# Attention with two-part float32r scores on array halves, and ten shared-expert batches between its steps

## The chip, the core and the metric

One NeuronCore of a Trainium2 runs the whole program. Its engines are TensorE (PE in the profile, its weight loads PEld), VectorE (DVE), ScalarE (ACT), GpSimd (POOL) and SyncE (SP, which only issues transfers). Each works through its own instructions in order and waits on semaphores. The metric is the device time of one execution in microseconds; lower is better.

## The reference

A gated cross attention and then a gated mixture of experts, on 32 batches of 128 rows by 512 columns (8 heads, 8 routed experts of which each token takes 2, and one shared expert), all in float32:

```python
q, k, v = proj(layernorm(x)), proj(ctx), proj(ctx)        # per batch, head size 16, sequence 512
attn = softmax(q @ k.T / 4)                               # 8 heads, 512 x 512
x = x + tanh(g_xattn) * (attn @ v)
h = rmsnorm(layernorm(x)) * rms_weight                    # 4096 tokens of 512
probs = softmax(h @ router_w); topv, topi = top_k(probs, 2); topv /= sum(topv)
moe = sum over the two experts e of topv[e] * (silu(h @ w_gate[e]) * (h @ w_up[e])) @ w_down[e]
sh = (silu(h @ sw_gate) * (h @ sw_up)) @ sw_down
out = x + tanh(g_ffn) * (moe + sh)
```

## The kernel before, in words

**Attention.** The main loop runs over turns i = -3 .. 31 and in each over 32 steps s (8 heads x 4 key tiles). In turn i, TensorE issues at step s one score matmul for the exponentials of batch i (`exp_scores`, L1033: keys on partitions, out to a bank of a ring of three, read by ScalarE in `exponential`, L892) and one for the row maxima of batch i+1 (`max_scores`, L1011: queries on partitions, out to another ring of three, read by VectorE in `maximum`, L696). float32 accuracy comes from splitting q and k into three bf16 parts stacked over the rows of the array: six products of 16 rows, 96 rows, and two more rows that subtract the maximum (98). At each step with s % 4 == 2 come four matmuls of probabilities with values (`values`, L1062, float32, each on 32 array columns). A float32 matmul stands in the trace as two instructions.

Other pieces stand at fixed steps and share one bank, `misc_ps`: projections of k and q of batch i+3 at steps 22 and 26 and of v of batch i+2 at step 7 (`project`, L996, L1000); transposes of the maxima at steps 18 and 2 (`turn_maxima`, L1020); the transpose of the tokens of batch i-3 and its router product at steps 10 and 14 (L1038, L1049).

**The parts.** ScalarE evacuates a projection and casts the high part, GpSimd subtracts for the middle and the low one (`split`, L523 to L526), SyncE writes the parts to DRAM and reads them back stacked.

**The denominators.** After the last value group of a batch, at step 2 of the next turn, ScalarE copies the sums (`take_values`, L899), SyncE stores them (`store_values`, L376), loads the denominators back spread over the partitions (L382), VectorE inverts them at step 13 (`invert`, L690), SyncE stores these (L386) and loads them with the sums for GpSimd (L392, L393), which adds the attention to x (`add_attention`, L533 to L535). GpSimd also refines inverse square roots by Newton steps (L503 to L505), normalises x (L514) and makes the tokens (`tokens`, L555, L556); SyncE stores these and their transposes to DRAM.

**The stage behind.** Jobs j = 0 .. 102: 32 shared-expert jobs, one a batch (16 gate and up matmuls, L1135, and the down product, L1160), then 71 routed jobs of 128 gathered tokens (L1140, L1148, L1160). During the shared jobs VectorE computes the routing in pieces, one a job; GpSimd scatters 64 columns of token numbers into a map in DRAM (L590), SyncE reads it back at job 28 (L483), TensorE transposes it at job 29 (L1100), and with these numbers GpSimd gathers tokens (L596). SyncE loads the routed experts' weights one at every second job from 5 on (L443).

The order is written out by hand: the constants at the top of the file give the steps and jobs.

## Time and profile before

| | us |
|---|---|
| median of 3 runs (lowest, highest) | 1590.97 (1590.81, 1591.98) |
| span of the profiled execution, first to last instruction | 1525.5 |
| TensorE busy in it | 1475.7 |
| GpSimd, VectorE, ScalarE busy | 814.5, 887.8, 782.5 |

The profile is of one execution. Busy time of an engine is the union of its instructions; where they overlap in its pipeline, starts are closer together than the length of one. "Idle before, releaser" is the time in which an engine waited ahead of a group, and whose end let it go. The chain of waits is followed back from the last instruction.

### The profile page before, as it was taken

To read this page: it belongs to the slowest core of one execution; us is meant where nothing else is said; L and a number is where in the kernel's file an instruction comes from. 1 tells how busy PE (TensorE), PEld (TensorE's weight loads), DVE (VectorE), ACT (ScalarE), POOL (GpSimd) and SP (SyncE) were. 2 spreads that over 40 slices of the span, in tenths; PEclk is the share of its full clock that TensorE was granted. 3 is DMA by queue.
4 is the path that set the end of the run, shared out by engine and by line. 5 is a ranking of instruction groups with operands and counts; after the bars stand their busy time and mean duration, and the time that the engine had idled before them with its cause. 6 is when DMAs were issued, how large, how long until landed. Compare 5 with 4: busy or idle time off the path is not lost.

```text
span 1525.5 us, 23419 instructions
## 1 busy us (share of the span) xinstructions
PE 1475.7 (97%) x7362; PEld 669.8 (44%) x7362; DVE 887.8 (58%) x1802; ACT 782.5 (51%) x1531; POOL 814.5 (53%) x1241
## 2 busy tenths in 40 slices
PE   5999999999999999999999999989999999999997
PEld 1233333333333333333333328767755454545443
DVE  5888888888888888888888842512221121211111
ACT  2577777777777777777777771100022222222221
POOL 6346675766757667576674443375134444444442
PEclk9999999999999999999999999999999999999999
DMA  6566667766676666765666424785345455554554
GB/s 153 128 160 168 175 167 183 180 161 162 162 177 163 168 163 162 178 170 152 165 154 167 117 92 162 248 213 121 113 76 97 85 96 88 93 91 88 92 90 61
DMA packets 159304, 215.10 MB, mean 141 GB/s; under 512 B 28162, under 2 KB 102416, under 8 KB 158160
## 3 DMA queue, kind: packets, MB, share of 16 engines
q1 hardware_dynamic: 137136, 175.78, 44.9%
q0 software_dynamic: 17952, 37.30, 14.0%
q8 instruction: 62, 1.02, 0.3%
q10 hardware_dynamic: 4096, 0.53, 0.2%
q14 instruction: 58, 0.48, 0.1%
HBM read 126.12 MB, written 86.91 MB: 140 GB/s over the span
## 4 chain that ended last, share of the span: by engine, by line
PE 87%; DMA 6%; DVE 2%; issue 1%; POOL 1%; ACT 1%; SPq 1%; ACTq 0%; POOLq 0%; DVEq 0%
PE bank L1140 16%; PE bank L1062 16%; PE bank L1033 14%; PE bank L1011 14%; PE bank L1160 10%; PE bank L1135 5%; PE bank L996 4%; PE bank L1038 3%; DMA arena<-ht_d 2%; PE bank L1049 2%; PE bank L1000 2%; DMA pv_d<-arena 1%; PE bank L1148 1%; DVE row_max L696 1%; PE bank L1020 1%
## 5 line engine op out<-in xcount | busy, mean ns | idle before, releaser
L696 DVE TENSOR_REDUCE row_max<-bank 128x1 f32<-128x512 f32 x1024 | 664.9, 682 | 111.6 <-PE bank L1011 102.5
L892 ACT ACTIVATE arena<-bank 128x512 f32<-128x512 f32 x1024 | 564.5, 612 | 205.5 <-PE bank L1033 194.0
L1011 PE MATMUL bank<-arena 96*128 96x512 bf16 x1024 | 392.2, 384 | 7.8 <-DVE row_max L696 5.5
L1033 PE MATMUL bank<-arena 98*128 98x512 bf16 x1024 | 387.2, 380 | 2.9 <-ACT arena L892 1.8
L1062 PE MATMUL bank<-arena 128*32 128x512 f32 x2048 | 272.7, 605 | 1.0 <-ACT arena L892 0.7
L1140 PE MATMUL bank<-arena 128*128 x568 | 255.5, 592 | 0.0
L834 DVE TENSOR_TENSOR arena<-arena,bank 128x256 f32<-128x256 f32 x103 | 43.4, 421 | 331.7 <-ACT arena L943 327.9
L943 ACT ACTIVATE arena<-bank 128x256 f32<-128x256 f32 x103 | 39.6, 384 | 378.2 <-PE bank L1140 224.9
L604 POOL DMA_INDIRECT out<-xs,ids x71 | 112.3, 1581 | 226.3 <-ACT xs L954 184.0
L1160 PE MATMUL bank<-arena 128*128 (+1 forms) x412 | 193.8, 593 | 0.9 <-ACT arena L959 0.9
L523 POOL TENSOR_TENSOR arena<-arena 128x512 bf16<-128x512 f32 x62 | 71.6, 1155 | 226.7 <-ACT arena L884 224.0
L1033 PEld LDWEIGHTS bank<-arena 98*128 98x128 bf16 x1024 | 102.2, 100 | 184.4 <-ACT arena L892 90.5
L1011 PEld LDWEIGHTS bank<-arena 96*128 96x128 bf16 x1024 | 100.2, 98 | 142.4 <-DVE row_max L696 80.7
L1140 PEld LDWEIGHTS bank<-arena 128*128 128x128 f32 x568 | 102.4, 190 | 101.9 <-issue 101.9
L1135 PE MATMUL bank<-arena 128*128 128x128 f32 x1024 | 121.9, 278 | 8.4 <-DMA arena<-ht_d 8.4
L1135 PEld LDWEIGHTS bank<-arena 128*128 128x128 f32 x1024 | 119.9, 194 | 21.2 <-DMA arena<-ht_d 13.0
L1160 PEld LDWEIGHTS bank<-arena 128*128 128x128 f32 x412 | 75.8, 190 | 84.4 <-issue 84.4
L822 DVE COPY arena<-bank 128x512 f32<-128x512 f32 x71 | 49.1, 691 | 104.3 <-PE bank L1038 104.3
L596 POOL DMA_INDIRECT xs<-h_d,ids x71 | 69.6, 980 | 56.1 <-DVE wts L862 34.8
L954 ACT ACTIVATE xs<-bank,wts 128x512 f32<-128x512 f32 x71 | 48.8, 687 | 95.5 <-PE bank L1160 56.8
L996 PE MATMUL bank<-arena 128*128 128x512 f32 x128 | 76.6, 682 | 15.8 <-POOL arena L514 9.7
L590 POOL DMA_INDIRECT map_d<-meta,slots x64 | 61.6, 962 | 50.1 <-DVE slots L805 30.9
(122 smaller groups left out, 1252.4 us busy)
## 6 DMA issues: line engine op xcount, KB each, us to landing
arena<-parts_q SPq DMA_DIRECT2D x64, 256.0 KB, 4.8
pv_d<-arena SPq DMA_DIRECT2D x32, 512.0 KB, 6.3
parts_k<-arena SPq DMA_DIRECT2D x96, 128.0 KB
arena<-parts_k SPq DMA_DIRECT2D x32, 384.0 KB, 4.9
parts_q<-arena SPq DMA_DIRECT2D x96, 128.0 KB
arena<-in_w SPq DMA_DIRECT2D x8, 1536.0 KB, 8.9
h_d<-arena SPq DMA_DIRECT2D x33, 256.0 KB, 6.7
out<-xs SPq DMA_DIRECT2D x33, 256.0 KB, 2.5
```

The costliest lines, as they stand in the source:

```text
L523: nc.gpsimd.tensor_tensor(mid, proj[n], hi, ALU.subtract).then_inc(s_part, 1)
L596: nc.gpsimd.indirect_dma_start(gathered[i % IN_RING], None, h_d, bass.IndirectOffsetOnAxis(ap=ids[:, i:i + 1], axis=0)).then_inc(s_got[i % ...
L604: nc.gpsimd.indirect_dma_start(out_d, bass.IndirectOffsetOnAxis(ap=ids[:, i:i + 1], axis=0), y_sb[i % OUT_RING], None, compute_op=ALU.add) ...
L696: nc.vector.reduce_max(row_max[b % 2][:, u:u + 1], m_ps[(STEPS * b + u) % M_BANKS][:], AX_X).then_inc(s_mx, 1)
L892: nc.scalar.activation(probs[group % 3][:, j, :], e_ps[n % E_BANKS][:], ACT.Exp, scale=float(DH) ** -0.5).then_inc(s_exp, 1)
L996: nc.tensor.matmul(misc_ps[:], (wk, wq)[n][:], ctx_in[b % 2] if n == 0 else xn[b % 2], start=True, stop=True).then_inc(s_proj, 1)
L1011: nc.tensor.matmul(m_ps[n % M_BANKS][:], q_stack[b % 3][0:STACK, h, qt * P:(qt + 1) * P], k_stack[b % 3][0:STACK, h, :], start=True, stop= ...
L1033: nc.tensor.matmul(e_ps[n % E_BANKS][:], k_stack[b % 3][0:SHIFTED, h, kt * P:(kt + 1) * P], q_stack[b % 3][0:SHIFTED, h, :], start=True, s ...
L1062: last = nc.tensor.matmul(pv_ps[2 * DH * j:2 * DH * (j + 1), :], v_ones[b % 3][:, kt, GROUP * g + j, :], probs[pair % 3][:, j, :], start=( ...
L1135: last = nc.tensor.matmul(G_PS[j % 2][:, f * P:(f + 1) * P], w_shared[:, c, f * P:(f + 1) * P], h_t[j % 3][:, c, :], start=(c == 0), stop= ...
L1140: last = nc.tensor.matmul(G_PS[j % 2][:], h_t[j % 3][:, c, :], routed_weights(j, c), start=(c == 0), stop=(c == CHUNKS - 1))
L1160: last = nc.tensor.matmul(Y_PS[j % 2][:], act_t[j % 2][:, f, :], w, start=(f == 0), stop=(f == FF // P - 1))
```

## The change

- Scores: q and k are split into two float32r parts (high and low). Three products of 16 rows are 48 rows (50 with the rows of the maximum), which fit in half of the array. Of a pair of heads one lies on partitions 0 to 63, the other on 64 to 127. At each step the exponentials' matmul takes one half and the maxima's the other.
- Bank rings per reader: `misc_ps` no longer serves the attention's pieces. Projections and token transposes take banks of the exponentials' ring (read by ScalarE), transposed maxima and router products banks of the maxima's ring (read by VectorE). Dictionaries `e_at` and `m_at` number their uses.
- Shared expert of batches 0 to 9 (`FUSED = 10`): in turns 3 to 12, the 16 gate and up matmuls stand in eight pieces of two at steps 7 to 17 and the down product in four at steps 24 to 29, in `misc_ps`. ScalarE takes a tanh and two copies, GpSimd four operations (silu is computed from tanh), SyncE stores the result. The stage behind has 22 shared jobs (`NS`), the map is read at job 19 and transposed at job 20, weights are loaded one a job. x is held for 22 batches.
- The maxima's rows go from VectorE (one negation) over GpSimd (two small operations) and SyncE's queue, before from VectorE (two) and ScalarE's queue. GpSimd makes the high part too, in place of ScalarE.
- SyncE's order in a turn is new, and the steps of the pieces are.

```diff
-K_PARTS = (HI, MID, LO, HI, MID, HI)
-Q_PARTS = (HI, HI, HI, MID, MID, LO)
+K_PARTS = (HI, LO, HI)
+Q_PARTS = (HI, HI, LO)
...
+PAIR = 2
+READS = PAIR * (len(runs(K_PARTS)) + len(runs(Q_PARTS)))
 STACK = len(K_PARTS) * DH
+SIDE = P // PAIR
...
+PROJECT_AT = {20: (3, 0), 28: (3, 1), 3: (2, 2)}
+MAX_AT = (19, 4)
 VALUES_LATE = 2
+TURN_TOKENS_AT = 1
+LOGITS_AT = 5
+GATE_UP_AT = {7: 2, 9: 2, 11: 2, 12: 2, 13: 2, 15: 2, 16: 2, 17: 2}
+DOWN_AT = (24, 25, 27, 29)
+HIDDEN_AT = 18
+SHARED_AT = 30
+MOMENTS2_AT = 3
 MOMENTS_AT = 23
 RECIP_AT = 13
+FUSED = 10
...
+        JOBS = NS + NT
+
+        EXPERT_JOBS = range(5, 5 + EXPERTS - 1)
...
+        LATE_AT = EXPERT_JOBS.stop + 2
+        MAP_AT = NS - 3
+        TURN_AT = NS - 2
...
             def split(b, n):
+                pool.wait_ge(s_er, e_at["project", b, n] + 1)
+                pool.wait_ge(s_wr[n], 2 * DMA * b)
+                hi, lo = parts[n]
+                nc.gpsimd.tensor_scalar(hi[:], proj[n], 1.0, 0.0, ALU.mult, ALU.add).then_inc(s_hi, 1)
                 pool.wait_ge(s_hi, 2 * b + n + 1)
...
+                nc.gpsimd.tensor_tensor(lo[:], proj[n], hi[:].bitcast(F32), ALU.subtract).then_inc(s_lo, 1)
...
+            def maxima_rows(b, half):
+                pool.wait_ge(s_mr, m_at["turn", b, half] + 1)
...
+                link(nc.gpsimd.tensor_scalar(rows[:, 0, :], m_neg[half][:], 1.0, 0.0, ALU.mult, ALU.add))
+                nc.gpsimd.tensor_tensor(rows[:, 1, :], m_neg[half][:], rows[:, 0, :].bitcast(F32), ALU.subtract
+                                        ).then_inc(s_mm, 1)
+
+            def activate_shared(b):
+                pool.wait_ge(s_ft, b + 1)
+                pool.wait_ge(s_fc, b + 1)
+                link(nc.gpsimd.tensor_scalar(half_tanh[:], half_tanh[:], 1.0, 0.5, ALU.add, ALU.mult))
+                link(nc.gpsimd.tensor_tensor(half_tanh[:], half_tanh[:], gate_and_up[:, 0:FF], ALU.mult))
...
             for i in TURNS:
                 if is_b(i + 2) and i + 2 > 0:
+                    split(i + 2, 0)
                     split(i + 2, 1)
+                if is_b(i):
+                    maxima_rows(i, 1)
+                if fused(i - 4):
+                    add_shared(i - 4)
                 if is_b(i + 4):
                     normalise(i + 4)
                 if is_b(i - 2):
                     tokens(i - 2)
-                if is_b(i + 3) and i + 3 > 0:
-                    split(i + 3, 0)
+                if is_b(i + 1):
+                    maxima_rows(i + 1, 0)
+                if fused(i - 3):
+                    activate_shared(i - 3)
                 if is_b(i - 1):
                     add_attention(i - 1)
...
+            def take_hidden(b):
+                act_e.wait_ge(s_fg, b + 1)
...
+                nc.scalar.activation(half_tanh[:], misc_ps[:, 0:FF], ACT.Tanh, scale=0.5).then_inc(s_ft, 1)
+                nc.scalar.copy(gate_and_up[:], misc_ps[:]).then_inc(s_fc, 1)
+
+            def take_shared(b):
+                act_e.wait_ge(s_fd, b + 1)
...
+                nc.scalar.activation(y_shared[:], misc_ps[:], ACT.Copy, scale=tgates[:, 1:2]).then_inc(s_fo, 1)
...
+            def next_e(at):
+                if at >= E_BANKS:
+                    pe.wait_ge(s_er, at - E_BANKS + 1)
+                return e_ps[at % E_BANKS]
+
+            def next_m(at):
+                if at >= M_BANKS:
+                    pe.wait_ge(s_mr, at - M_BANKS + 1)
+                return m_ps[at % M_BANKS]
...
             def max_scores(b, u):
...
+                p, qt, e = u // (PAIR * KT), u // PAIR % KT, 1 - u % PAIR
+                rows = slice(e * SIDE, e * SIDE + STACK)
...
+                ps = next_m(m_at["max", b, u])
+                nc.tensor.matmul(ps[:], q_stack[b % 3][rows, p, qt * P:(qt + 1) * P],
+                                 k_stack[b % 3][rows, p, :], start=True, stop=True).then_inc(s_mf, 1)
...
             def exp_scores(b, s):
                 g, kt, j = s // (GROUP * KT), s // GROUP % KT, s % GROUP
...
+                p, e = GROUP // PAIR * g + j // PAIR, j % PAIR
+                rows = slice(e * SIDE, e * SIDE + SHIFTED)
...
+                ps = next_e(e_at["exp", b, s])
+                nc.tensor.matmul(ps[:], k_stack[b % 3][rows, p, kt * P:(kt + 1) * P],
+                                 q_stack[b % 3][rows, p, :], start=True, stop=True).then_inc(s_ef, 1)
...
+            def shared_hidden(b, units):
...
+                for unit in units:
+                    f, c = divmod(unit, CHUNKS)
+                    last = nc.tensor.matmul(misc_ps[:, f * P:(f + 1) * P], w_shared[:, c, f * P:(f + 1) * P],
+                                            tok_t[:, c, :], start=(c == 0), stop=(c == CHUNKS - 1))
```

How the orders move, at three places. The first is TensorE at steps 7 to 10 of a turn in which a shared batch is worked in. Before (L1033 exponentials, L1011 maxima, L1000 projection of v, L1062 values, L1038 tokens):

```order
L1033 MATMUL bank1<-arena 128x512
L1011 MATMUL bank3<-arena 128x512
L1000 MATMUL bank7<-arena 128x128 x4
L1033 MATMUL bank2<-arena 128x512
L1011 MATMUL bank4<-arena 128x512
L1033 MATMUL bank0<-arena 128x512
L1011 MATMUL bank5<-arena 128x512
L1033 MATMUL bank1<-arena 128x512
L1011 MATMUL bank3<-arena 128x512
L1062 MATMUL bank6<-arena 32x512 x4
L1038 MATMUL bank7<-ident,arena 128x128 x4
```

After (L1141 exponentials, L1120 maxima, L1184 gate and up, L1209 values):

```order
L1141 MATMUL bank2<-q_stack0,k_stack0 128x512
L1120 MATMUL bank3<-k_stack1,q_stack1 128x512
L1184 MATMUL bank7<-arena 128x128 x2
L1141 MATMUL bank0<-q_stack0,k_stack0 128x512
L1120 MATMUL bank4<-k_stack1,q_stack1 128x512
L1141 MATMUL bank1<-q_stack0,k_stack0 128x512
L1120 MATMUL bank5<-k_stack1,q_stack1 128x512
L1184 MATMUL bank7<-arena 128x128 x2
L1141 MATMUL bank2<-q_stack0,k_stack0 128x512
L1120 MATMUL bank3<-k_stack1,q_stack1 128x512
L1209 MATMUL bank6<-arena 32x512 x4
```

The projection and the tokens have gone to steps 3 and 1, and two pieces of the shared expert, on all 128 rows, stand between scores that now take 64 rows each.

The second is SyncE from the store of the sums to the load of the denominators. Before (L367 reads of k, L376 store of the sums, L357 writes of q's parts, L382 load of the denominators, L386 store of their inverses):

```order
L367 DMA arena<-parts_k1 16x8x512
L376 DMA pv_d<-arena 128x2x512
L357 DMA parts_q1<-arena 8x16x512
L382 DMA arena<-pv_d 128x1x32
L357 DMA parts_q1<-arena 8x16x512
L386 DMA rden_d<-arena 128x32
```

After (L396 write of a part, L418 store of the sums, L374 and L369 loads of the next inputs, L453 rows of the maxima, L409 reads of k, L424 load of the denominators):

```order
L396 DMA parts_q1<-q_lo 8x16x512
L418 DMA pv_d<-arena 128x2x512
L374 DMA arena<-in_ctx 128x512
L369 DMA xs<-in_x 128x512
L453 DMA q_stack0<-m_rows1 2x8x128 x2
L409 DMA k_stack2<-parts_k1 32x4x512 x2
L409 DMA k_stack2<-parts_k1 16x4x512 x2
L424 DMA arena<-pv_d 128x1x32
```

The store has gone behind all writes of parts, and between it and the load stand two inputs, the rows of the second half's maxima and four reads of k.

The third is the end of SyncE's turn. Before (L386 store of inverses, L332 input, L403 transposed tokens, L367 reads of q, L392 and L393 loads for the attention sum, L397 store of tokens):

```order
L386 DMA rden_d<-arena 128x32
L357 DMA parts_q1<-arena 8x16x512
L332 DMA arena<-in_ctx 128x512
L403 DMA ht_d<-arena 128x512
L367 DMA arena<-parts_q1 16x8x512 x2
L367 DMA arena<-parts_q1 32x8x512 x2
L392 DMA arena<-rden_d 128x1x512
L393 DMA arena<-pv_d 128x1x512
L397 DMA h_d<-arena 128x512
```

After (L458 store of a finished shared batch, L428 store of inverses, L439 store of tokens, L434 and L435 loads for the attention sum, L453 rows of the first half's maxima):

```order
L458 DMA out<-xs 128x512
L428 DMA rden_d<-arena 128x32
L439 DMA h_d<-arena 128x512
L434 DMA arena<-rden_d 128x1x512
L435 DMA arena<-pv_d 128x1x512
L453 DMA q_stack1<-m_rows0 2x8x128 x2
```

The store of the tokens now stands ahead of the loads for the attention sum, and the rows of the maxima have come onto this queue.

## Rows read from the trace of the kernel before

**Rows 1.** the page: span, busy us (share) by engine, one group (busy us, mean ns)

```profile
span 1525.5 us, 23419 instructions
...
PE 1475.7 (97%) x7362; PEld 669.8 (44%) x7362; DVE 887.8 (58%) x1802; ACT 782.5 (51%) x1531; POOL 814.5 (53%) x1241
...
L696 DVE TENSOR_REDUCE row_max<-bank 128x1 f32<-128x512 f32 x1024 | 664.9, 682 | 111.6 <-PE bank L1011 102.5
```

**Rows 2.** table by stretch: us; PE, PEld, DVE, ACT, POOL busy; clock; DMA

```profile
500.00:600.00 100.00, 99.95 (x559) 36.46 (x559) 85.98 (x177) 76.96 (x148) 64.50 (x111) 1.00 0.67 169
```

**Rows 3.** timeline of TensorE in one turn: start us, length us, what, how many

```profile
501.71 0.38 PE L1011 MATMUL bank<-arena 96*128 96x512 bf16 x1
502.02 1.07 PE L1062 MATMUL bank<-arena 128*32 128x512 f32 x8
503.02 0.28 PE L1020 MATMUL bank<-ident,row_max 128*16 128x128 f32 x1
...
530.16 0.28 PE L1020 MATMUL bank<-ident,row_max 128*16 128x128 f32 x1
```

**Rows 4.** the chain of waits in the same turn: start us, us, what

```profile
504.60 0.22 PE bank L1033
...
505.04 1.00 PE bank L1062 x8
506.04 1.06 PE bank L996 x2
...
513.63 0.32 PE bank L1033
```

**Rows 5.** the chain of waits behind the turns, shared jobs to first routed

```profile
914.94 3.59 PE bank L1135 x32
...
927.57 5.51 DMA arena<-pv_d
...
1041.71 3.57 PE bank L1135 x32
1045.28 1.72 PE bank L1160 x4
...
1084.03 0.18 PE bank L1100 x2
...
1101.01 3.44 PE bank L1140 x8
```

**Rows 6.** timeline of ScalarE in the turn: five exponentials back to back

```profile
513.67 2.58 ACT L892 ACTIVATE arena<-bank 128x512 f32<-128x512 f32 x5
```

**Rows 7.** timeline of VectorE in the turn: reciprocals and maxima

```profile
499.71 0.35 DVE L690 RECIPROCAL arena<-arena 128x32 f32<-128x32 f32 x1 [0.62 <-DMA arena<-pv_d]
...
514.21 2.48 DVE L696 TENSOR_REDUCE row_max<-bank 128x1 f32<-128x512 f32 x4 [0.23 <-PE bank L1011]
...
526.15 0.34 DVE L690 RECIPROCAL arena<-arena 128x32 f32<-128x32 f32 x1
```

**Rows 8.** timeline of SyncE in the turn: store of values, load of denominators

```profile
518.03 0.38 SPq L376 DMA_DIRECT2D pv_d<-arena  x1
...
524.03 0.61 SPq L382 DMA_DIRECT2D arena<-pv_d  x1
```

**Rows 9.** timeline of GpSimd in the turn: idle, big operations, start of normalising

```profile
510.24 1.15 POOL L523 TENSOR_TENSOR arena<-arena 128x512 bf16<-128x512 f32 x1 [6.14 <-ACT arena L884]
...
515.20 0.77 POOL L534 TENSOR_SCALAR arena<-arena,tgates,tg_bv 128x512 f32<-128x512 f32 x1
516.04 1.27 POOL L535 TENSOR_TENSOR xs<-xs,arena 128x512 f32<-128x512 f32 x1
...
521.00 0.34 POOL L503 TENSOR_SCALAR newton<-rstd,arg 128x1 f32<-128x1 f32 x1
...
524.35 0.77 POOL L514 TENSOR_SCALAR arena<-xs,rstd,nmr 128x512 f32<-128x512 f32 x1
```

**Rows 10.** the scatters into the map: ns min/median/max, first and last start us

```profile
L590 POOL DMA_INDIRECT map_d<-meta,slots x64: 954/958/1236, 975.5 to 1055.3; - x64
```

## What the change does to the time: the prediction

> **What bounds the kernel now.** Read the page first [rows 1]: TensorE is busy 97% of a 1525.5 us span. Busy matmuls prove little, so next comes one table by stretches [rows 2]: from 500 to 600 us TensorE is busy all the time at the full granted clock, VectorE 86%, ScalarE 77%, GpSimd 65%. Then one period of the attention loop (a turn): the transpose of the first half of the next batch's maxima starts at 503.02, that of the next turn at 530.16 [rows 3], so a turn takes 27.14 us, and 31 of the 32 take that (the last has no next batch to take maxima for). The chain of waits says of what [rows 4]: a score matmul costs 0.22 us, a group of eight value instructions 1.00. 64 score matmuls at 0.218 make 14.0 us; the other 13.2 are eight value groups, three projections, the transposes of maxima and tokens, and the router. Nothing waits in between. Behind the turns come 32 shared jobs at 3.57 + 1.72 = 5.29 us [rows 5] and then 71 routed jobs, which the change leaves alone.
>
> The median is 1590.97 us, the profiled span 1525.5; the 65.5 us between lie outside the span and are taken as unchanged, so every difference below is added to 1590.97.
>
> **The scores.** The count stays at 64 a turn and the columns at 512. What changes is the type (bf16 to float32r) and the rows: 48 or 50, at partition 0 or 64, and each exponential's matmul stands beside a maximum's on the other half. No row shows a float32r matmul. Nearest from below is the bf16 one, 0.22 us; from above the float32 projection of 512 columns, 1.06 us with its switch, in two instructions [rows 4]. Nor does a row show two array halves at work together, but the values show the like for columns: eight instructions of 512 columns on four 32-column strips take 1.00 us, where two such instructions alone take 1.06, so strips do overlap. I take the near end, 0.22 us a matmul and two at once: 32 x 0.22 = 7.0 us a turn in place of 14.0. Ends for the range: 14.0 (halves one after the other, or half rate), and 64 x 1.06 / 2 = 34.
>
> The Trainium skill, Perfetto Trace Analysis, Engine Utilization, halves the array's rate only for FP32_LOW_HIGH among four-byte types; that is for the near end, and no row here shows it.
>
> **Switches.** Into a value group the step is 0.31 us instead of 0.22 (501.71 to 502.02) [rows 3], and the matmul behind one costs 0.32 [rows 4]: 0.19 a round trip. Score matmuls now use half the rows, so every full-array piece between them makes such a trip too: 7 a turn (three projections, two maxima, tokens, router): 1.3 us. TensorE then needs 7.0 + 13.2 + 1.3 = **21.5 us** in a plain turn.
>
> The rule that speaks against the change is in TensorEngine Tiling (Array Packing), Tiling Modes, of the Trainium skill: changing the mode, not just the tile, drains the array. The 0.09 and 0.10 above agree in kind. If a drain instead exposed all of a matmul's 0.38 us beyond its 0.22 [rows 3], a trip would cost 0.32, a turn with shared pieces 19 x 0.13 = 2.5 us more, and the sum would end 25 us later.
>
> **The shared expert moved in.** Ten of 31 turns take in one shared batch: 5.3 us of matmuls, in 8 + 4 pieces, so 12 more trips (2.3). TensorE: 21.5 + 5.3 + 2.3 = **29.1 us**. ScalarE gets three activations more there and loses two casts in every turn; it is busy 0.77 x 27.14 = 21 us of a turn now, and back to back five exponentials take 2.58 us [rows 6], so that it stays below 29.
>
> **What is late next: VectorE.** One maximum lasts 0.68 us [rows 1], but four back to back end after 2.48, so a next one comes every (2.48 - 0.68) / 3 = 0.60 us [rows 7]. 32 of them 19.2, two statistics over as many columns 1.3, a reciprocal 0.35, and the negations and small ones about 1.6 (an estimate, at most what is left of the 86% of 27.14 us after 32 x 0.60): **22.4 us**. So in a plain turn TensorE (21.5) hands the bound to VectorE.
>
> **The denominators.** Then a path shows that 27.14 us hides. It starts with the last value group of the batch before (step 2), runs through ScalarE's copy, SyncE's store of the values, its load of the denominators, and ends in VectorE's reciprocal, which stands at step 13 ahead of all later maxima. Times [rows 4, 7, 8]: values 1.0, copy 0.6 (as an exponential), store 6.0 (518.03 to 524.03), load 2.1 (524.03 to 526.15), reciprocal 0.35: 10.1 us. The reciprocal at 499.71 already waited 0.62 us for it. From step 13 to the next step 2 VectorE has 21 maxima (12.6), a negation and a set of moments (1.4): 14.0. Together 24.1 us, above VectorE's 22.4. The store now also stands behind the four writes of parts, and the load behind the maxima's rows and four reads of k, all on SyncE.
>
> **GpSimd's loop.** Its order closes a second loop, since SyncE stores the tokens ahead of the loads for the attention sum. From [rows 9]: two splits, each a scalar operation and a subtraction with the gaps between, 2 x (0.8 + 1.4) = 4.4; rows of maxima about 0.8 (an estimate, two operations at 0.34 for a tiny one); normalising 3.35 + 0.8 = 4.1; tokens 3.35 + 0.8 + 1.3 = 5.4; then three issues and a landing (0.4 + 0.6 + 5.5 [rows 5]) 6.5, beside which lie the next rows and the activation; adding attention 2 x 1.27 + 0.77 and gaps, 3.6. Sum 24.8 us. Before, this loop was not closed: GpSimd sat idle 6.14 us ahead of 510.24. The two loops meet at the store (it waits for the second split), which I put at half a microsecond. Plain turn: **25.3 us**. Fused turn: the pieces lengthen steps 2 to 13 by about 3 us, so both paths hide under TensorE: 29.1 + 0.2 = **29.3**.
>
> 31 turns before: 31 x 27.14 = 841. After: 21 x 25.3 + 10 x 29.3 = 531 + 293 = 824. **17 us gained.** Filling the pipeline (memsets of 2048 columns that lie under the first loads, one part less to split) and the last turn: 0, bounds -5 and +5.
>
> **The stage behind.** Ten jobs less are 53 us of matmuls, but a path of other work ends last there. GpSimd issues 64 scatters from 975.5 to 1055.3, 1.27 us each [rows 10]; the last ends 141 us after the first shared matmul at 914.94; its landing and the map's load take 5 more. From the map's transposes to the first routed matmul there are two jobs, a gather and so on: 1084.03 to 1101.01, 17 us [rows 5]. 146 + 17 = 163 us against 186 before. SyncE's load of the map stands ahead of the tokens of jobs 20 and 21, so TensorE stands idle there, about 20 us. The weight loads come every job instead of every second: +2. So **21 us gained**, not 53.
>
> Sum: 17 + 21 = 38, and 1590.97 - 38 = **1553 us**.
>
> **Rivals.**
> - Quick: the paths through SyncE and GpSimd don't bind, and switches are cheap. Plain 23.0, fused 28.0: 841 - 763 = 78, + 21: 1492 us. For: landing times of 2.1 us in the loads; against: the wait of 0.62 us that is there already.
> - Slower, the halves take turns (or four-byte rows go in at half rate): the scores stay at 14.0 us. Plain 14.0 + 13.2 + 1.3 = 28.5, fused 36.1: 841 to 959, + 118 - 21: 1688 us; with free switches (27.14 and 32.4) 1623. Middle 1660. It decides from 0.34 us a pair on: there plain turns take 14.5 + 32 x 0.34 = 25.4 and fused 33.0, and 10 x 5.9 - 21 x 1.7 = 23 eats the gain behind the turns. For: the values overlap in columns, never in rows, and no row has a four-byte operand at one pass. Against: nothing else in the trace.
> - SyncE late: landings grow as more bytes fall into a shorter turn, plain 27: 841 - 860, 21 gained behind: 1589 us.
> - float32r priced as float32: 34 + 14.5 a turn, over 2200 us.
>
> **How the numbers follow.** Forecast 0.50 (1515 to 1585), quick 0.15, turns taken 0.25, SyncE late 0.06, float32 price 0.04. The range 1470 to 1665 leaves out a twentieth below and some 0.13 above. Within 0.2% (3 us, what a measurement can tell): 0.03, from where the forecast and the late SyncE reach the old time. Slower 0.30, faster 0.67.
>
> **What would show it.** Pairs of score matmuls with starts close together and a new pair each 0.22 us (right) or single ones 0.22 apart (the slower rival). Plain turns near 25 with VectorE waiting for a DMA at its reciprocal; fused ones near 29 with TensorE full. Behind the turns one long idle stretch of TensorE until the map lands, and 163 us from the first shared to the first routed matmul. Plain turns at 23 would refute both loops; fused turns over 31 the price of a switch.

## The result, and the profile after

The changed kernel takes 1765.47 us (median of four runs), the kernel before 1590.89 on the same chips: 1.107 times as long, 95% interval 1.101 to 1.113. The ratio leaves out the slowest of the four executions (1782.72 us), which lies over 1.5% above the fastest. **Slower by 11%**, where 1553 us were forecast and 1665 was the upper end.

The page of the kernel after, against [rows 1]; its first lines, then TensorE's busy tenths and its granted clock in 40 slices of 44 us:

```profile
span 1750.0 us, 23258 instructions
PE 1576.1 (90%) x7402; PEld 739.2 (42%) x7402; DVE 877.2 (50%) x1716; ACT 780.6 (45%) x1487; POOL 795.4 (45%) x1347
PE   3999999999999998998899899994198999999997
PEclk7688997999998787798888999996599999999999
```

TensorE is busy 100 us longer than before, although it now does 32 pairs a turn in place of 64 single score matmuls. And its clock, full in [rows 2], is now below nine tenths in 14 of the first 26 slices.

Matmuls of a fused turn at full clock (start, length, engine, line; L1141 makes the exponentials' scores, L1120 the maxima's, L1184 is a gate and up piece, L1209 a value group):

```profile
430.92 0.50 PE L1141 MATMUL bank<-q_stack,k_stack 50*128 50x512 f32 x1
430.92 0.50 PE L1120 MATMUL bank<-k_stack,q_stack 48*128 48x512 f32 x1
431.35 0.71 PE L1184 MATMUL bank<-arena 128*128 128x128 f32 x4
432.00 0.50 PE L1141 MATMUL bank<-q_stack,k_stack 50*128 50x512 f32 x1
...
436.61 0.49 PE L1141 MATMUL bank<-q_stack,k_stack 50*128 50x512 f32 x1
436.62 0.73 PE L1120 MATMUL bank<-k_stack,q_stack 48*128 48x512 f32 x2
436.95 0.40 PE L1141 MATMUL bank<-q_stack,k_stack 50*128 50x512 f32 x1
437.28 1.06 PE L1209 MATMUL bank<-arena 128*32 128x512 f32 x8
438.27 0.49 PE L1141 MATMUL bank<-q_stack,k_stack 50*128 50x512 f32 x1
```

The two matmuls of a pair start together, so the halves do overlap. But the next pair starts 0.34 us later (436.61 to 436.95), not 0.22, and a pair alone between two pieces on the full array takes 0.43 (430.92 to 431.35). The piece then takes 0.65 for four matmuls of 128 columns.

The 0.34 is the price of the first pair behind a piece only. Where three pairs stand in a row (L1146 transposes tokens), the first takes 0.33 us (515.81 to 516.14) and the second 0.24 (to 516.38):

```profile
514.81 1.06 PE L1209 MATMUL bank<-arena 128*32 128x512 f32 x8
515.81 0.49 PE L1141 MATMUL bank<-q_stack,k_stack 50*128 50x512 f32 x1
515.81 0.73 PE L1120 MATMUL bank<-k_stack,q_stack 48*128 48x512 f32 x2
516.14 0.64 PE L1141 MATMUL bank<-q_stack,k_stack 50*128 50x512 f32 x2
516.38 0.40 PE L1120 MATMUL bank<-k_stack,q_stack 48*128 48x512 f32 x1
517.08 0.63 PE L1146 MATMUL bank<-ident,arena 128*128 128x128 f32 x4 [0.30 <-ACT arena L981]
```

Over all pairs at full clock from 150 to 1000 us the medians are 0.234 us for a further pair ahead of a pair, 0.338 for the first one behind a piece, 0.330 for a further one ahead of a piece and 0.431 for one alone between two pieces. So a pair costs 0.234, and a piece adds 0.10 to the pair behind it and 0.10 to the pair ahead of it.

A plain turn:

```profile
662.01 0.79 PE L1141 MATMUL bank<-q_stack,k_stack 50*128 50x512 f32 x1
662.01 1.22 PE L1120 MATMUL bank<-k_stack,q_stack 48*128 48x512 f32 x2
662.60 1.05 PE L1141 MATMUL bank<-q_stack,k_stack 50*128 50x512 f32 x2
665.27 1.38 PE L1120 MATMUL bank<-k_stack,q_stack 48*128 48x512 f32 x2 [1.62 <-DVE row_max L789]
665.87 0.62 PE L1141 MATMUL bank<-q_stack,k_stack 50*128 50x512 f32 x1
666.59 1.93 PE L1209 MATMUL bank<-arena 128*32 128x512 f32 x8
```

Here the value group takes 1.86 us (to 668.45), against 1.00 at full clock, and TensorE waits for a bank that VectorE has not read. VectorE's rows tell why (waits over eleven turns, 565.3 to 932.9: total, times, longest):

```profile
DVE row_max L789 <- PE bank L1120: 84.2, 109, 2.0
DVE arena L782 <- DMA arena<-pv_d: 25.4, 9, 7.6
```

L782 is the reciprocal: it waited 0.62 us before [rows 7], now up to 7.6. The same eleven turns by stretches (us, busy and count of TensorE, its weight loads, VectorE, ScalarE, GpSimd, then clock, DMA share, GB/s):

```profile
565.30:932.90 367.60, 336.69 (x1691) 130.49 (x1693) 254.39 (x506) 221.53 (x415) 177.99 (x374) 0.83 0.55 143
```

A plain turn is 33.4 us, where it was 27.1.

**Where the 160 us lie.** A second profile of the kernel before (e0 below) has a span of 1589.6 us, in which the first shared matmul stands at 916.9 and the first routed one at 1165.2. After: 1117.6 and 1326.2. So attention is 200.6 us longer, the shared jobs 39.6 shorter (208.7 for 248.3), the routed part the same (423.8 for 424.4): 160.4, the difference of the spans.

Within attention, from reciprocal to reciprocal: the first comes 13.6 us later (clock at half from 19 to 77). Eleven periods up to 497.2 take 389.7 us where 11 x 27.1 = 298 stood; the next sixteen, to 1025.5, take 528.3 against 434. The last four are 3 us longer.

### The profile page after: what moved, and what is told of

Its sections match the earlier page's. It is cut to its first block and busy times, and to the rows that moved or that the text cites. A ratio compares the mean times of both kernels' runs of the same rounds, so it can differ in the third digit from the quotient of the medians.

```text
span 1750.0 us, 23258 instructions
## 1 busy us (share of the span) xinstructions
PE 1576.1 (90%) x7402; PEld 739.2 (42%) x7402; DVE 877.2 (50%) x1716; ACT 780.6 (45%) x1487; POOL 795.4 (45%) x1347
## 5 line engine op out<-in xcount | busy, mean ns | idle before, releaser
L1120 PE MATMUL bank<-k_stack,q_stack 48*128 48x512 f32 x1024 | 476.1, 522 | 44.7 <-DVE row_max L789 33.4
L1141 PE MATMUL bank<-q_stack,k_stack 50*128 50x512 f32 x1024 | 454.3, 504 | 12.3 <-ACT arena L981 11.4
L1141 PEld LDWEIGHTS bank<-q_stack,k_stack 50*128 50x128 f32 x1024 | 190.9, 205 | 400.4 <-ACT arena L981 276.5
L1209 PE MATMUL bank<-arena 128*32 128x512 f32 x2048 | 312.0, 685 | 0.8 <-ACT arena L981 0.7
L1120 PEld LDWEIGHTS bank<-k_stack,q_stack 48*128 48x128 f32 x1024 | 194.4, 207 | 77.8 <-DVE row_max L789 61.4
L1052 ACT ACTIVATE arena<-bank 128x256 f32<-128x256 f32 x93 | 35.6, 383 | 403.3 <-PE bank L1293 225.0
L1313 PE MATMUL bank<-arena 128*128 (+1 forms) x372 | 178.7, 602 | 8.0 <-issue 7.1
L599 POOL TENSOR_SCALAR m_rows<-m_neg 16x128 fp32r<-16x128 f32 x64 | 18.4, 288 | 359.7 <-issue 181.2
L1288 PE MATMUL bank<-arena 128*128 128x128 f32 x704 | 96.3, 291 | 54.7 <-issue 53.4
L1293 PEld LDWEIGHTS bank<-arena 128*128 128x128 f32 x568 | 102.4, 190 | 101.9 <-issue 101.9
L1288 PEld LDWEIGHTS bank<-arena 128*128 128x128 f32 x704 | 91.4, 206 | 66.0 <-issue 62.5
L1313 PEld LDWEIGHTS bank<-arena 128*128 128x128 f32 x372 | 70.0, 193 | 89.0 <-issue 89.0
L1106 PE MATMUL bank<-arena 128*128 128x512 f32 x128 | 86.1, 760 | 17.1 <-POOL arena L574 12.1
```

The costliest lines, as they stand in the source:

```text
L1106: nc.tensor.matmul(ps[:], (wk, wq)[n][:], ctx_in[b % 2] if n == 0 else xn[b % 2], start=True, stop=True).then_inc(s_ef, 1)
L1120: nc.tensor.matmul(ps[:], q_stack[b % 3][rows, p, qt * P:(qt + 1) * P], k_stack[b % 3][rows, p, :], start=True, stop=True).then_inc(s_mf, 1)
L1141: nc.tensor.matmul(ps[:], k_stack[b % 3][rows, p, kt * P:(kt + 1) * P], q_stack[b % 3][rows, p, :], start=True, stop=True).then_inc(s_ef, 1)
L1209: last = nc.tensor.matmul(pv_ps[2 * DH * j:2 * DH * (j + 1), :], v_ones[b % 3][:, kt, GROUP * g + j, :], probs[pair % 3][:, j, :], start=( ...
L1288: last = nc.tensor.matmul(G_PS[j % 2][:, f * P:(f + 1) * P], w_shared[:, c, f * P:(f + 1) * P], h_t[j % 3][:, c, :], start=(c == 0), stop= ...
L1293: last = nc.tensor.matmul(G_PS[j % 2][:], h_t[j % 3][:, c, :], routed_weights(j, c), start=(c == 0), stop=(c == CHUNKS - 1))
```

## The experiments

All fifteen in one table. "Attention" is the start of the first shared matmul, "fused" and "plain" are mean periods of the reciprocal over six turns with and eleven turns without shared pieces, and the clock is the mean over these eleven (1.00 is 2.4 GHz, 0.50 is 1.2 GHz). The last column is the kernel before on the same chip.

| kernel | us | attention | fused | plain | clock | before |
|---|---|---|---|---|---|---|
| after | 1751.8 | 1117.6 | 36.0 | 33.4 | 0.83 | |
| e0 before again | 1591.4 | 916.9 | | 27.1 | 1.00 | 1584.3 |
| e1 reciprocal late | 1799.5 | 1167.1 | 35.6 | 33.7 | 0.87 | 1584.3 |
| e2 one half only | 2627.9 | | 73.5 | 56.1 | 0.50 | 1584.3 |
| e3 full rows | 1726.4 | 1093.3 | 34.3 | 32.5 | 0.97 | 1584.3 |
| e4 bfloat16 halves | 1706.8 | 1072.6 | 32.6 | 32.7 | 0.89 | 1585.8 |
| e5 load first | 1782.8 | 1151.2 | 35.2 | 33.9 | 0.85 | 1585.8 |
| e6 full rows, load first | 1745.6 | 1112.5 | 34.4 | 33.9 | 0.96 | 1585.8 |
| e7 sixteen fused | 1750.5 | 1148.9 | 36.2 | (33.9, mixed) | 0.92 | 1585.8 |
| e8 no trip | 1659.4 | 1058.9 | 35.5 | 28.5 | 0.98 | 1533.9 |
| e9 full rows, no trip | 1635.7 | 1037.0 | 34.4 | 29.2 | 1.00 | 1533.9 |
| e10 rows first | 1715.1 | 1117.4 | 35.6 | 32.2 | 0.88 | 1533.9 |
| e11 bfloat16, rows first | 1676.5 | 1077.2 | 33.3 | 32.5 | 0.87 | 1533.9 |
| e12 before, half the scatters | 1551.2 | 916.4 | | 27.2 | 1.00 | 1588.5 |
| e13 bfloat16, no trip | 1630.1 | 998.7 | 32.6 | 29.1 | 0.93 | 1588.5 |
| e14 after again | 1761.1 | 1129.9 | 36.2 | 33.6 | 0.84 | 1588.5 |

Each row is one execution; the two profiles of the changed kernel (after, e14) lie 12 us apart in attention. Whole times compare only on one chip: that of e8 to e11 runs the kernel before in 1533.9 us, the others in 1584 to 1589, for a reason that stands outside the attention (e12). So attention is compared by its own column.

### e0 and e12: the 65 us that the first profile did not show

> The kernel before, unchanged, profiled a second time. Two readings of the 65 us between its profiled span (1525.5 us) and its median. (a) They lie outside the span, as the prediction put it: the span is near 1525 again. (b) They lie inside the span of most executions, as a stretch in the shared expert's jobs in which TensorE gets one matmul every 2.8 us, as the changed kernel's profile has it from 1190 to 1266 us: the span is near 1589, and the stretch stands there while GpSimd issues the scatters.

Reading (b) is right: the span is 1589.6 us. One row of each table by stretches, first the old profile, then e0:

```profile
1000.00:1050.00 50.00, 45.21 (x309) 36.51 (x309) 9.38 (x16) 3.07 (x8) 38.07 (x40) 1.00 0.83 181
```

```profile
1000.00:1050.00 50.00, 7.79 (x21) 6.04 (x21) 0.42 (x1) 0.38 (x1) 38.05 (x40) 0.50 0.02 1
```

GpSimd issues its scatters at the same pace in both, but in e0 TensorE gets 21 matmuls where it got 309, and almost nothing is transferred. Its rows in e0:

```profile
1025.20 0.37 PE L1135 MATMUL bank<-arena 128*128 128x128 f32 x1 [2.43 <-issue]
1028.00 0.37 PE L1135 MATMUL bank<-arena 128*128 128x128 f32 x1 [2.43 <-issue]
1030.80 0.37 PE L1135 MATMUL bank<-arena 128*128 128x128 f32 x1 [2.43 <-issue]
```

e12 leaves out every second scatter of the kernel before:

```diff
-                for t in range(B):
+                for t in range(0, B, 2):
                     nc.gpsimd.indirect_dma_start(map_d, ...)
...
-                    sp.wait_ge(s_sc2, 2 * B * DMA)
+                    sp.wait_ge(s_sc2, B * DMA)
```

> The kernel before with half of its 64 scatters into the map (every second batch's slots are left out, so the routed part works on a map with holes; its work is the same in size). Theory (the scatters make the stretch in which TensorE gets one matmul every 2.8 us): the stretch is half as long, 30 to 40 us instead of about 70, and the span about 30 us shorter than that of the kernel before on the same chip. Rival (the stretch comes from the jobs of the shared expert or from the chip, not from the scatters): its length and the span stay within 10 us.

The scatters now end at 1017.5 instead of 1056.5, and the slow stretch with them; two rows of e12:

```profile
1000.00:1025.00 25.00, 7.34 (x21) 5.30 (x21) 1.07 (x2) 0.38 (x1) 14.17 (x15) 0.50 0.02 1
1025.00:1050.00 25.00, 25.00 (x158) 19.94 (x157) 5.13 (x10) 1.92 (x5) 0.00 (x0) 0.95 0.66 232
```

From the first shared to the first routed matmul it is 208.6 us for 248.3: 39.7 less. The stretch goes with the scatters. Why TensorE's instructions come slowly then ("issue": nothing that the profile shows), and why one profile and one chip are free of it, stays open. The changed kernel has it too (78.5 us at half clock from 1196).

### e1, e5, e10: moving the late link

e1 is one number, `RECIP_AT = 13` to `22`.

> The changed kernel with the reciprocal placed nine steps later in VectorE's turn (22 for 13). Theory (the reciprocal's wait for the denominators holds up VectorE, with it the maxima's banks and TensorE, and the halved clock of the plain turns comes from such waits): the waits of 3.3 to 7.6 us are gone, turns go from 33.5 to about 29.5 us, the granted clock in plain turns is over 0.95, and the whole is near 1640 us. Rival (the clock falls because score matmuls on half the rows do not keep it up): the waits go, the clock stays at 0.8 to 0.88, turns are near 32 us and the whole 1700 to 1720.

The reciprocal's waits went, and nothing was won: plain turns 33.7. TensorE now waited for something else (600 to 800 us, total, times, longest):

```profile
PE bank L1141 <- DMA q_stack<-m_rows: 21.1, 10, 5.0
```

SyncE's store of the reciprocals waits for VectorE, and the next batch's rows of maxima stand behind it in SyncE's order. Both theories fall: the clock did not recover (0.87, within the rival's 0.8 to 0.88), but turns did not shorten by the rival's 1.5 us either.

e5 issues the load of the denominators earlier (e6 is the same edit on e3):

```diff
+                if is_b(i):
+                    row(i, 1)
+                if is_b(i - 1):
+                    load_denominators(i - 1)
                 if is_b(i + 4) and i + 4 >= 2:
                     load_ctx(i + 4)
                 if is_b(i + X_AHEAD):
                     load_x(i + X_AHEAD)
-                if is_b(i):
-                    row(i, 1)
                 if is_b(i + 2):
                     read(i + 2, 0)
-                if is_b(i - 1):
-                    load_denominators(i - 1)
```

> The changed kernel with another order on SyncE: behind the store of the value sums come the rows of maxima, then at once the load of the denominators, and only then the loads of context and x and the first read of a stack. It is issued about 3 us earlier in the turn. Theory (TensorE in the plain turns is held up by the reciprocal that waits for the denominators, 3 to 7 us in a turn): those waits and TensorE's idle time behind the maxima go, plain turns get 1.5 to 3 us shorter, the whole is near 1700. Rival (the waits only take up time that the halved clock leaves): the waits go, the plain turns stay at 33, the whole stays within 15 us of 1750.

The DMA wait of VectorE fell to 18.3 us in twelve turns, turns stayed at 33.9. SyncE's rows of e5 (600 to 1000 us) tell where it went:

```profile
SPq L434 <- DMA rden_d<-arena: 75.7, 12, 7.2
SPq L424 <- DMA pv_d<-arena: 29.1, 11, 3.6
```

The store of 16 KB of reciprocals now lands behind eight stack reads: 6 us of waiting a turn (after: 43.3 us in 16 turns from 550 to 1100, 2.7 each), and SyncE also waits for the store of the values.

e10 puts the reciprocal at step 20 and on SyncE `row(i + 1, 0)` ahead of `store_reciprocals(i - 1)`.

> The changed kernel with the reciprocal at step 20 of VectorE's turn instead of 13, and on SyncE the rows of maxima of the first half ahead of the store of the reciprocals, not behind the load of the values. Theory: neither VectorE nor the rows wait for the round trip any more; the trip has slack; plain turns go from 33.3 to 30 us or less, the whole to about 1690. Rival (GpSimd, which now gets the values 3 us later, is next: the parts of k and q come late): turns stay at 33, the whole within 15 us of 1750.

Attention ended at 1117.4, against 1117.6: nothing won again (the 37 us in the whole time are the other chip's). From 600 to 1000 us GpSimd waited 123.3 us, thirteen times, for the values, rows of maxima came late behind that, and TensorE waited 22.2 us for them. Three places for the same link, three times 32 to 34 us. We read this as a ring whose length counts, not its order; e8 tests it.

### e8, e9: without the trip

e8 loads and stores reciprocals for the first batch only (`if b: return` in `load_denominators` and `store_reciprocals`; `load_values` waits for the store of the values, the reciprocal for the first load alone).

> The changed kernel without the round trip of the denominators: only those of the first batch are loaded, inverted into DRAM and used, for all batches; the value sums still go out and come back. Theory 1 (a plain turn of 33 us is held by that round trip, issued by SyncE between rows of maxima, stacks and values): turns fall to TensorE's own work, 26 to 28 us plain at full clock, and with few waits the clock holds; the whole is near 1620. Theory 2 (the clock falls because half-row matmuls do not keep it up, waits or not): the waits go, but the clock in the plain turns stays at or below 0.85, turns are 29 to 31 us, the whole near 1680. Both leave the fused turns at 34.4.

> The run with every score matmul on all 128 rows, and also without the round trip of the denominators, as in e8. TensorE's own work is 29 us of a plain turn there. Theory: with the trip gone its plain turns are 29 to 30 us at full clock, the fused ones 34.4, and the whole is near 1660 (1725 less 20 turns of 3 us). Rival (something else in the turn is as long as the trip): plain turns over 31.5 us, the whole over 1700. Against e8 it shows at equal terms what the halves give or cost: if e8 has the lower clock, this one is within 2% of it, or faster.

Eleven plain turns each, e8 first, then e9:

```profile
564.80:878.70 313.90, 289.97 (x1702) 117.71 (x1694) 254.16 (x507) 221.34 (x419) 177.05 (x371) 0.98 0.63 164
```

```profile
532.90:853.60 320.70, 316.65 (x1702) 170.84 (x1694) 253.56 (x508) 221.83 (x419) 177.39 (x375) 1.00 0.63 164
```

Theory 1 holds: e8's plain turns are 28.5 us on average, five of the eleven 27.3 and the longest 30.7, and the clock is nearly full (0.98). The trip held the turn; since e8 takes away its waits and its transfers together, it does not say which of them did. The half clock came only in part with waits. All four falls of the clock in e8's rows follow a wait of TensorE of 1.3 to 2.2 us. Of the twelve in the eleven turns of after, seven begin behind a wait of over 1 us; in the 7 us before each of the other five (the one at 653.8, for instance) TensorE waited 0.33 us at a time at most. e9's turns are 29.15 us, one like the other, as long as TensorE's own work. The whole of e8 came 40 us above the forecast, and that on a chip without the slow stretch of the scatters, since attention still ends 142 us after that of the kernel before: fused turns stay at 34.34 to 34.38, two stretches at the low clock, from 199 and from 486 us, lengthen four periods to 39 to 41, and the start is slow. At equal terms the kernel with full rows ends its attention 22 us earlier, with one execution of each. It loses 0.6 us in each plain turn and wins more at the start and in the four long periods: what the halves save in the plain turns, the low clock takes back.

### e2, e3, e4, e13: what a pair costs

e3 gives every score matmul all 128 rows (`rows = slice(0, P)`), with the rows of maxima at zero, so that no two can overlap and no change of mode stands beside the full-array pieces.

> The changed kernel with every score matmul on all 128 rows, still float32r: each head of a pair gets the sum of both heads' products, and the rows of maxima are zero. No two matmuls can lie beside each other, and no change of array mode stands before the pieces on the full array. Theory (changes of mode and the clock they take are most of the loss, and float32r streams as fast as bfloat16): 0.22 us a score matmul, full clock throughout, plain turns 27 to 28 us, fused turns 33, the whole near 1620. Rival (the loss lies in the order of SyncE and GpSimd and in the reciprocal's wait): turns stay over 31 us and the whole over 1700.

Its rows, to be held against those of after at 430.92:

```profile
404.17 0.61 PE L1186 MATMUL bank<-arena 128*128 128x128 f32 x4
404.54 0.48 PE L1143 MATMUL bank<-q_stack,k_stack 128*128 128x512 f32 x1
404.85 0.39 PE L1122 MATMUL bank<-k_stack,q_stack 128*128 128x512 f32 x1
405.08 0.38 PE L1186 MATMUL bank<-arena 128*128 128x128 f32 x2
```

Two score matmuls and a piece: 0.54 + 0.37 = 0.91 us with all rows, 0.43 + 0.65 = 1.08 us in halves. So wherever such a piece stands between two pairs the halves lose 0.17 us; between bare pairs they win (0.34 for the first and 0.24 for further ones, against 2 x 0.234). Summed over a fused turn at full clock, each step from start to next start (e8, halves, six turns from 253 us; e9, all rows, seven from 195 us):

| us a turn | scores | value groups | all other pieces | sum |
|---|---|---|---|---|
| halves (e8) | 13.0 | 8.0 | 12.8 | 33.7 |
| all rows (e9) | 19.2 | 8.0 | 6.9 | 34.1 |

The halves save 6.2 us in the scores and lose 5.9 in the nineteen pieces between them: a gate and up piece takes 0.64 us for 0.36, a down piece 0.63 for 0.24, a projection of k or q 1.06 for 0.46. So the turn comes out even: 34.4 us in both. e3 was still 24 us better in attention (37 against e14), with a clock of 0.97 in place of 0.83. Its plain turns, 32.5, stayed over 31: it has the trip as well, and the rival's "over 1700" was right.

e4 reads only the upper two bytes of each element (`.bitcast(BF16)[:, 1::2]`) on the same halves.

> The changed kernel with bfloat16 operands for the scores: each score matmul reads only the upper two bytes of every float32r element, on the same half of the rows, so the scores are rounded to bfloat16 and the rest is the same. Theory A (a pair of 0.34 us is bound by its two weight loads of four-byte elements, 0.205 us each, where the kernel before had 0.10): a pair goes to about 0.22 us, fused turns from 34.4 to near 31 us, and the whole to about 1680 if the waits of the plain turns allow it. Theory B (the price is that of a half with its change of mode, whatever the type): a pair stays at 0.33 and the time within 20 us of 1750. In both, the clock of the plain turns stays under 0.9, since the rows in use are the same.

```profile
437.75 0.40 PE L1141 MATMUL bank<-q_stack,k_stack 50*128 50x512 bf16 x1
437.75 0.62 PE L1120 MATMUL bank<-k_stack,q_stack 48*128 48x512 bf16 x2
437.99 0.39 PE L1141 MATMUL bank<-q_stack,k_stack 50*128 50x512 bf16 x1
438.30 1.07 PE L1209 MATMUL bank<-arena 128*32 128x512 f32 x8
```

The first pair is 0.24 us (437.75 to 437.99), as theory A had it, and one alone between two pieces 0.33, where it was 0.43. Further pairs stay as they were (median 0.229 for 0.234). So the four-byte type costs 0.10 us once behind every piece, not in every pair. It shows in the weight loads. Their groups from 600 to 900 us, after and then e4 (busy us, mean ns, idle before):

```profile
L1120 PEld LDWEIGHTS bank<-k_stack,q_stack 48*128 48x128 f32 x284 | 55.2, 214 | 25.4 <-DVE row_max L789 24.8
```

```profile
L1120 PEld LDWEIGHTS bank<-k_stack,q_stack 48*128 48x128 bf16 x296 | 23.9, 95 | 58.7 <-DVE row_max L789 55.3
```

At full clock (400 to 500 us) the float32r load is 183 ns. The Trainium skill, TensorE: Matmul & The Clock Gate, Weight-path perf modes, says that the fast weight load wants 128 weights and a type other than FP32. These rows agree if float32r counts as FP32, 183 to 214 ns against 95.

But the loads do not set the pace of every pair. The two of a pair run side by side, and those of the next pair begin 0.11 us later:

```profile
436.61 0.18 PEld L1141 LDWEIGHTS bank<-q_stack,k_stack 50*128 50x128 f32 x1 [0.76 <-ACT arena L981]
436.61 0.29 PEld L1120 LDWEIGHTS bank<-k_stack,q_stack 48*128 48x128 f32 x2
436.72 0.19 PEld L1141 LDWEIGHTS bank<-q_stack,k_stack 50*128 50x128 f32 x1
```

A load that nothing covers behind a piece would explain a surcharge that comes once. That is argued, not shown: e4 changes the type of the streamed operand along with that of the weights, and no run changes one alone.

e4 won 45 us of attention: 29 in the first eleven periods, 5 at the start, and 10 in the next sixteen (33.4 to 32.7 in the eleven of the table), since the trip holds them. e13 takes the trip away too:

> The changed kernel with bfloat16 operands for the scores (as in e4) and without the round trip of the denominators (as in e8). If float32r costs 0.1 us a pair and nothing covers it any more, plain turns go from 27.3 (e8) to about 24.1 us and fused ones from 34.4 to 31.2: attention ends near 960 us instead of 1059. If another wait is next (rows of maxima, GpSimd's 25 us), plain turns stay at 26 or over.

Attention at 998.7, 60 us ahead of e8. Fused turns were 32.1 and not 31.2; of the plain ones the shortest were 25.7, but the mean 29.1, at a clock of 0.93. So a quicker TensorE did not get its 24 us: the low clock came back. TensorE's waits of over 1 us were 21.8 us in these eleven turns, 8.2 in e8; what made them, we did not test. e11 (e4 with e10's order) repeats e10:

> The order of e10 with the bfloat16 operands of e4 (scores rounded to bfloat16). If the trip alone held e4's plain turns at 32 us, they fall to 26 to 28 us and the whole from 1707 to about 1620; if the clock or GpSimd holds them, they stay over 30 and the whole over 1680.

Attention 1077.2, e4 had 1072.6: the order gives nothing.

e2 puts both matmuls of a pair on partitions 0 to 49.

> The changed kernel with all score matmuls on partitions 0 to 49: the odd heads get the even heads' scores, and the counts are the same. Theory (the halves overlap and save 0.1 us a pair): a pair goes from 0.34 to 0.44 us, turns get 3 us longer, 1750 becomes 1840. Rival (a pair is bound by its two weight loads of 0.205 us each, and the overlap saves nothing): a pair takes 0.34 to 0.43 us and the time is within 20 us of 1750.

Neither. Five fused turns of e2, 73.5 us each:

```profile
544.18:911.68 367.50, 367.50 (x972) 166.02 (x971) 123.32 (x231) 119.25 (x205) 95.88 (x190) 0.50 0.25 66
```

TensorE was busy without a gap in these turns, and its clock stayed at 0.50 from 21.2 to 1994.1 us, of which it was busy 1958. The overlap does save: between a value group and a piece the two matmuls take 1.15 us in e2 (602.75 to 603.90), where after at the same clock takes 0.72 (668.45 to 669.17). What they would cost at full clock this run cannot say, and most of its loss is the clock.

### e6, e7, e14

> The run with every score matmul on all 128 rows (sums of both heads' products, rows of maxima zero), and with the load of the denominators moved ahead as in e5. There the clock is near full in the plain turns and TensorE's own work about 29 us of 32. Theory: its plain turns fall to 29 to 30 us and the whole from 1725 to about 1680; the fused turns, bound by TensorE, stay at 34.4. Rival (another wait of the same size is next, the rows of maxima or the values for the residual): plain turns over 31 us, the whole over 1710.

The rival again: TensorE waited 21.1 us (twelve turns) for rows of maxima, plain turns 33.9, worse than e3.

e7 is `FUSED = 16`.

> The changed kernel with the shared expert of sixteen batches in the attention turns instead of ten. Theory (the pieces on the full array hold the clock at its upper level, and cost TensorE 5 to 8 us of a turn that otherwise goes to the lower clock and waits): six more turns are at 34.4 us where they took 33.3, about +7 us, and the stage behind is six batches shorter at 5.8 us each, about -35; the whole is near 1722. Rival (each fused turn costs its full 7 us): the whole is near 1757.

Attention 31.3 us longer (5.2 for each batch moved in), the shared stage 33.1 us shorter (175.6 for 208.7): nothing won, as the rival says (it put 7 us on a batch). Turns with pieces have the higher clock (0.92 for 0.83 over the same eleven), but they remain TensorE's own 34.3.

> The changed kernel, unchanged, profiled again beside e12 and e13. Attention should end within 20 us of its first profile (1117) and plain turns take 33 to 34 us. If the stretch of one matmul every 2.8 us is a matter of the chip, both kernels show it here or neither: with it the stage from the first shared to the first routed matmul is near 208 us, without it near 173, as in e8 to e11.

1129.9 and 33.6: the first profile was no exception. Its stage behind took 205.4 us, on a chip that runs the kernel before in 1588.5.

## Why the prediction was wrong

**Which step failed first.** "0.19 a round trip", the price of a switch, with which "TensorE then needs 7.0 + 13.2 + 1.3 = **21.5 us** in a plain turn". The rate of the pairs was nearly right: 0.234 us against 0.22, two at once, in a run of pairs. But a turn has few runs. In a fused turn 23 of the 32 pairs stand alone between two pieces at 0.43 us, so the scores take 13.0 us (e8, 253 to 459 us). That is 32 x 0.234 = 7.5 and 27 times 0.20, for all 27 pieces, value groups too. The kernel before took 14.8 by the same count.

And a switch also lengthens the piece, for which the sum had nothing: its 0.19 was read from the steps of score matmuls around a value group, and a value group itself takes 1.00 us at full clock in the kernel before, in after and in e9. The twelve shared pieces take 7.65 us and not 5.3. With their 12 x 0.20 in the scores a trip around one of them costs 0.40. The other seven pieces sum with the values to 13.1, where the kernel before has 12.3 and 0.9 for switches in its scores (the 13.2 of the forecast).

In plain turns pairs fall apart as well. Of e8's, those of 27.3 us at full clock have 37 starts for 32 pairs: some score matmuls start without their partner, as at 665.27 behind a wait for a bank. Their scores take 12.8 us where 32 x 0.234 + 15 x 0.20 = 10.5 would do. TensorE's plain turn is 12.8 + 13.1 = 25.9 us and not 21.5, and 1.4 us of waits come on top. The overlap was right, its worth was not. The slower rival decides from plain turns of 25.4 us and fused ones of 33.0 on; with 25.9 and 33.7 of TensorE's work its side was reached, by another mechanism: the halves did not take turns.

**The denominators.** This is the second step that failed: the mechanism was right and named, but both terms of its 24.1 us were too small. From the last value group to the end of the reciprocal 10.1 us were forecast: in the turn at 683.67 it took 15.3. Its links on SyncE, store and load (start, length, line):

```profile
687.40 0.37 SPq L418 DMA_DIRECT2D pv_d<-arena  x1
...
690.45 1.78 SPq L409 DMA_DIRECT2D k_stack<-parts_k  x4
692.33 0.64 SPq L424 DMA_DIRECT2D arena<-pv_d  x1
...
698.97 0.34 SPq L428 DMA_DIRECT2D rden_d<-arena  x1
```

The copy was 3.1 us behind the group, the load 4.9 behind the store, and it landed 6.3 us later, behind four stack reads, where 2.1 were taken from [rows 8]. The rest, "from step 13 to the next step 2 ... 14.0 together", was reckoned at VectorE's pace; these maxima come at TensorE's, and that half of the turn was 19.0 us (34.3 - 15.3). Ring 34 instead of 24.1.

**The clock is in no term.** Busy time per plain turn of after is 336.7 / 11 = 30.6 us, the clock's share of it (1 - 0.83) x 33.4 = 5.7, and idle (367.6 - 336.7) / 11 = 2.8. That leaves 25 of own work, as above. By e8 5 us a turn hang on the trip, clock included: 33.4 - 28.5.

**Fused turns.** Forecast 7.0 + 13.2 + 1.3 + 5.3 + 2.3 = 29.1. Measured 13.0 + 13.1 + 7.65 and 0.6 idle: 34.4. Of the 4.6 us more in TensorE's work about 2.5 are the switches of the shared pieces (7.65 + 2.4 for 5.3 + 2.3), 1.4 the scores with the other switches, and 0.8 the older pieces. "Fused turns over 31 refute the price of a switch" was a good test: they did, and that price was wrong.

**The shared stage.** Forecast 21 us shorter; 39.6 on equal terms. Where the scatters' stretch is missing, 172 to 174.5 us lie between first shared and first routed matmul (e8 to e11), near the 163 of the sum. Without it the kernel before has 186.0 (its first profile), so the gain would be 12 to 14 us, less than the 21 of the forecast. The stretch costs the kernel before 62 us (248.3 less 186.1) and the changed one about 35, as far as two chips may be compared. That was not foreseen: 27 of the 39.6 us come from it.

**The 65.5 us outside the span.** Wrong (e0): timed runs have 1.8 us outside. With it the forecast would have been some 27 us lower, the 62 less 35 by which the stretch is shorter in the changed kernel.

**The other rivals.** SyncE late had the right mechanism at 27 us a turn instead of 33. GpSimd's loop of 24.8 was not reached, nor was VectorE's floor of 22.4 (the shortest plain turn is 25.7, e13).

**Sum.** Attention was forecast 17 us shorter and came out 201 longer. Ten fused turns at 34.3 for 27.1 are 72 of the 92 us in the first eleven periods; low clock and waits are the other 20. The sixteen plain ones lost 94: 16 x (28.5 - 27.1) = 22 with the trip away (e8), and 16 x 4.5 = 72 by trip and clock. 14 are the start.

e1, e5, e7 and e10 keep the whole computation, and none brought the attention or the sum nearer to the kernel before; nothing we found beats it.

## What to carry to other kernels

When packed matmuls stand between pieces on the full array, count the runs of pairs, not the pairs: the rate inside a run (0.234 us here) was nearly as forecast, and the switches around 27 pieces made up the loss. Price a switch on both sides, in the packed matmuls and in the piece, and read it from a piece of the kind that will stand there. When a change takes TensorE's work away, write down each round trip whose issue and use are tied to fixed steps of its loop, with landings taken from transfers that have the same neighbours in the queue, and the loop's part at the pace of the engine that really feeds it. If moving a link three ways leaves the period, take the whole trip out once: that tells in one run what the order could at best give. And profile the baseline twice before a gap between span and median is explained.

## What the hardware showed that I had not expected

- Pairs of float32r matmuls on 48 and 50 rows at full clock: 0.234 us in a run, 0.10 more for the first behind a full-array piece and 0.10 more ahead of one. With bfloat16 operands 0.229, and only 0.01 more for the first. The weight loads: 183 ns and 95 to 100.
- The same pieces on the full array take longer between pairs on halves than between matmuls on all rows: 0.64 for 0.36 us (four matmuls of 128 columns), 0.63 for 0.24 (two of 256). A group of eight on 32-column strips takes 1.00 in both.
- In these runs the clock fell with score matmuls on half of the rows where it hardly did with all rows. At nearly the same busy share, 92%, and nearly the same waits of over 1 us (17.4 and 17.7 us in eleven plain turns) the clock is 0.83 in after and 0.97 in e3; e6, on all rows with 33.8 us of such waits, has 0.96. e8 has 0.98 with halves too, at 8.2 us of such waits. e2, with all scores on one half, has 0.50 for 1973 us. The Trainium skill, TensorE: Matmul & The Clock Gate, Part 1, ties the clock to how busy TensorE is. In e2 the profile counts it busy 99% of that time, at the lower level: here the measurement goes beyond the page.
- While GpSimd issues 64 scatters (80 us), TensorE may get one matmul every 2.8 us and transfers nearly stop (1 GB/s), in most executions but not in all. It stays open why.
